# Four edits to a graph-network kernel on one core: bias copies, bf16 adjacency rows, casts on GpSimd, a merged first loop

## The chip, the core and the metric

One core of a Trainium2 chip runs the whole program. The metric is the device time in microseconds (us), lower is better. The core has a matrix engine (TensorE, PE in the rows), its weight loads (PEld), VectorE (DVE), ScalarE (ACT), GpSimd (POOL) and a queue engine (SyncE, SP) that here issues nearly all DMAs. The engines meet only at semaphores.

## The reference, cut to what matters

2708 nodes with 256 features are padded to 22 blocks of 128 (NT = 22). Four graph layers follow one another, each behind a layer norm and a ReLU with a residual sum; the fourth is run only if a test on the adjacency values asks for it, and here it does not.

```
# layer 0: attention of 4 heads of 64 columns over all neighbours
ht = (h @ Wm).reshape(n, 4, 64); el, er = ht . al, ht . ar
attn = softmax(where(adj == 0, -inf, leaky_relu(el[:, None] + er[None, :])))
out = attn @ ht
# layer 1: two GRU cells around an attention of 3 heads
node_support = (adj without diagonal) @ h
edge_output = gru(node_support, h, edge_Wih, edge_Whh, edge_bih, edge_bhh)
edge_support = mean over 3 heads of softmax(where(adj > 0, e_plus[None, :], NEG)) * adj @ (h @ W_head)
node_output = gru(edge_support, h, node_Wih, node_Whh, node_bih, node_bhh)
out = de * edge_output + dn * node_output
# gru(x, h): r, z = sigmoid(x @ Wih.T + bih + h @ Whh.T + bhh); n = tanh(xn + bin + r * (hn + bhn)); (1-z) n + z h
# layer 2: out = concat(h, adj @ h / (deg + 1)) @ W.T
```

## The kernel before, in words

The order of work on every engine is written out by hand: each engine has one stream of instructions with waits on named semaphores, and a wait holds everything behind it on that engine. The adjacency is held in AT as fp8, one block row per source block j.

**Layer 0.** First the features are normed and multiplied (L1628, L1641), and GpSimd casts the first 6 of the 22 column blocks of each adjacency row from f32 in STG to fp8 in AT (L693). Then comes a loop over the 22 source blocks that makes MOV, the operand of the attention products as two f16 halves: VectorE multiplies (L1145, `t_b`), GpSimd multiplies (L707, `t_d`), ScalarE rounds to the high half (L851), VectorE subtracts to the low half (L1139, `mov`). Only when all 22 are made do the attention units start. There are 12 units, 3 column groups of 6, 8 and 8 blocks times 4 heads, each with 22 steps j; unit n and step j make m = 22 n + j. One step: a threshold tile (fp8) of the scores, on ScalarE (L869) or VectorE (L1161) as `threshold_on_act` says, then two masks on VectorE (L1193 and, by xor, L1199), then four matmuls of 65 columns for each block (L1674). Of the thresholds, ScalarE makes all of unit 0, 13 of 22 in units 1 to 7 and 18 in units 8 to 11. At j = 8 ScalarE evicts the unit before (L881) and VectorE normalizes it (L1208 to L1214, `head_out`). ScalarE also casts the 44 adjacency tiles of the second and third column group (L859), spread over units 0 to 7 by `casts_at`. In units 8 to 11 VectorE widens the adjacency (L1220) and GpSimd clears its diagonal blocks (L715). The scores of a unit are loaded by SP (`load_el`) two units ahead.

**Layer 1, edge loop.** 22 blocks t. Per block PE does half of a support product (L1720, 44 matmuls of 256 columns), the head products (L1732, L1734), and the gates of the GRU (`gru_mm`): 12 matmuls of 512 columns (L1759), one of 3 rows that adds the bias (L1761), then twice 6 of 256 columns (L1766), each with a bias matmul (L1767). ScalarE takes tanh of the gates (L940), VectorE combines (L1388, L1390), ScalarE takes tanh (L942), GpSimd subtracts (L728, `delta`), VectorE blends (L1397, L1398), GpSimd adds to X (L733, L734, `apply`). VectorE also splits support and products into halves (L1342, L1348, L1351). Between these VectorE takes row maxima (L1366): each of the 3 heads needs, for 22 rows in two halves, the maximum of the adjacency half row (f32, 704 KB, loaded from the input for every head anew, three buffers AROW) times the scores of the head (EB). Of the 132 maxima 44 are done by block 13 (`ROWS_SPLIT`), 73 by the end of the loop (`ROWS_EDGE`), the rest at every second step of the attention. GpSimd clears the diagonal block of one half of each row first (L743). In block 20 the maxima of head 0 are turned on PE (L1778), copied (L1379), saved and reloaded broadcast (`save_maxima`, `load_maxima`); the first attention unit needs them.

**Layer 1, attention.** 9 units of 22 steps. Per step: exponents (L952 on ScalarE or L1409 on VectorE), a mask (L1419), powers (L961), and 2 matmuls of 257 columns for each block (L1812, L1813). Six pieces of the next weights are split on GpSimd (L675 to L677). The node bias is summed and split in three bf16 parts on VectorE at m = 118 to 120 (L1271 to L1282). VectorE counts sensitive entries (L1471) from m = 122.

**Node GRU and layer 2.** 22 blocks of `gru_mm` again, with ScalarE's `node_high` (L993), VectorE's `support_half` (L1526), norm statistics (L1062) and, from block 10, the linear product of layer 2 (L1853) in between. Then the neighbour sums (L1866).

## Time and profile before

| what | us |
|---|---|
| median of the runs (3) | 1363.55 |
| lowest, highest | 1361.31, 1370.84 |
| the profiled execution's own time | 1376.85 |
| its span (first to last instruction) | 1375.0 |
| granted TensorE clock, mean over the span | 0.935 of full |
| busy in the span: PE, VectorE, ScalarE, GpSimd | 1187.0, 1000.2, 759.6, 267.6 |

The rows further down come from that one execution; times in them are us from the start of its span. In a timeline row the first number is the start, the second the duration, and a bracket at the end tells how long the engine was idle before and what released it. VectorE's instructions overlap a little at their ends, so the distance between two starts is what one costs.

### The profile page before, as it was taken

To read this page: it belongs to the slowest core of one execution; us is meant where nothing else is said; L and a number is where in the kernel's file an instruction comes from. 1 tells how busy PE (TensorE), PEld (TensorE's weight loads), DVE (VectorE), ACT (ScalarE), POOL (GpSimd) and SP (SyncE) were. 2 spreads that over 40 slices of the span, in tenths; PEclk is the share of its full clock that TensorE was granted. 3 is DMA by queue.
4 is the path that set the end of the run, shared out by engine and by line. 5 is a ranking of instruction groups with operands and counts; after the bars stand their busy time and mean duration, and the time that the engine had idled before them with its cause. 6 is when DMAs were issued, how large, how long until landed. Compare 5 with 4: busy or idle time off the path is not lost.

```text
span 1375.0 us, 36177 instructions
## 1 busy us (share of the span) xinstructions
PE 1187.0 (86%) x15179; PEld 944.5 (69%) x15179; DVE 1000.2 (73%) x2281; ACT 759.6 (55%) x1142; POOL 267.6 (19%) x340
## 2 busy tenths in 40 slices
PE   4518897999868999999966999997899998988996
PEld 3418897999757766566635888886788654446885
DVE  6587997999985676676776999898995365553641
ACT  3469987998752122222116999896989225553000
POOL 4730000032041022332231110111210042220000
PEclk9759999999975999999977999999999999999998
DMA  9715553211015667768679778676762000020532
GB/s 319 240 70 170 180 148 119 81 34 65 3 49 210 211 205 252 245 215 285 223 251 344 228 247 329 208 248 210 257 223 101 1 28 20 16 92 1 190 107 84
DMA packets 88623, 223.59 MB, mean 163 GB/s; under 512 B 7427, under 2 KB 52345, under 8 KB 88197
## 3 DMA queue, kind: packets, MB, share of 16 engines
q1 hardware_dynamic: 87269, 220.68, 48.5%
q8 instruction: 121, 1.98, 0.6%
q10 hardware_dynamic: 1184, 0.53, 0.1%
q14 instruction: 49, 0.40, 0.1%
HBM read 201.45 MB, written 19.73 MB: 161 GB/s over the span
## 4 chain that ended last, share of the span: by engine, by line
PE 52%; DMA 15%; DVE 14%; ACT 8%; POOL 5%; issue 4%; SPq 1%; DVEq 0%; ACTq 0%; POOLq 0%
PE PS L1674 12%; DMA arena<-in_adj 12%; PE PS L1812 10%; PE PS L1813 10%; PE PS L1866 8%; ACT arena L869 3%; PE PS L1759 3%; DVE scratch L1366 3%; PE PS L1853 2%; PE PS L1766 2%; DVE arena L1139 1%; ACT AT L859 1%; POOL X L734 1%; PE PS L1709 1%; DVE arena L1199 1%
## 5 line engine op out<-in xcount | busy, mean ns | idle before, releaser
L1812 PE MATMUL PS<-arena 128*128 128x257 f16 x1452 | 331.5, 276 | 27.3 <-ACT arena L961 21.6
L1813 PE MATMUL PS<-arena 128*128 128x257 f16 x1452 | 331.3, 278 | 0.0
L1674 PE MATMUL PS<-arena 128*128 128x65 f16 x7744 | 261.8, 196 | 76.1 <-DVE arena L1199 61.4
L1674 PEld LDWEIGHTS PS<-arena 128*128 128x128 fp8e4 x7744 | 258.1, 99 | 79.7 <-issue 59.0
L1366 DVE CUSTOM_DVE_ANT_0 scratch<-arena 128x1408 bf16<-128x1408 f32 x132 | 216.9, 1643 | 84.1 <-DMA arena<-in_adj 48.5
L961 ACT ACTIVATE arena<-arena 128x896 int16<-128x896 uint8 (+1 forms) x198 | 187.4, 972 | 36.3 <-DVE arena L1419 27.5
L869 ACT ACTIVATE arena<-arena 128x1024 fp8e4<-128x1024 f32 (+1 forms) x185 | 189.9, 1089 | 17.7 <-DVE arena L1193 16.9
L1812 PEld LDWEIGHTS PS<-arena 128*128 128x128 bf16 x1452 | 144.2, 99 | 52.8 <-ACT arena L961 18.1
L1813 PEld LDWEIGHTS PS<-arena 128*128 128x128 bf16 x1452 | 141.6, 97 | 23.1
L952 ACT ACTIVATE arena<-arena,E1B 128x896 uint8<-128x896 f32 (+1 forms) x131 | 139.2, 1063 | 13.6 <-DMA arena<-m_rows 13.6
L942 ACT ACTIVATE arena<-arena 128x256 f32<-128x256 f32 x44 | 18.3, 416 | 205.0 <-DVE arena L1390 205.0
L1193 DVE TENSOR_TENSOR arena<-arena,AT 128x256 int32<-128x256 int32 (+1 forms) x264 | 104.8, 397 | 25.3 <-ACT arena L869 18.2
L1759 PE MATMUL PS<-arena 128*128 128x512 f16 x528 | 123.0, 383 | 0.0
L1720 PE MATMUL PS<-AT,arena 128*128 128x256 fp8e4 x968 | 112.1, 276 | 0.0
L1866 PE MATMUL PS<-arena,AT 128*128 128x256 f16 x968 | 106.2, 273 | 0.8 <-DVE X L1520 0.8
L1199 DVE TENSOR_TENSOR arena<-arena,AT 128x256 int32<-128x256 int32 (+1 forms) x264 | 104.1, 395 | 0.0
L1720 PEld LDWEIGHTS PS<-AT,arena 128*128 128x128 f16 x968 | 94.2, 99 | 14.0
L1866 PEld LDWEIGHTS PS<-arena,AT 128*128 128x128 fp8e4 x968 | 94.6, 98 | 12.5 <-DVE X L1520 1.1
L743 POOL TENSOR_TENSOR arena<-arena,NOTI 128x128 f32<-128x128 f32 x66 | 46.0, 697 | 286.2 <-DMA arena<-in_adj 286.1
L1759 PEld LDWEIGHTS PS<-arena 128*128 128x128 f16 x528 | 52.3, 99 | 56.5 <-issue 2.5
L1419 DVE TENSOR_TENSOR arena<-arena,AT 128x224 int32<-128x224 int32 (+1 forms) x198 | 79.8, 428 | 10.8 <-ACT arena L952 10.6
L728 POOL TENSOR_TENSOR arena<-arena 128x256 f32<-128x256 f32 x44 | 32.8, 745 | 256.1 <-ACT arena L942 256.1
(192 smaller groups left out, 1570.7 us busy)
## 6 DMA issues: line engine op xcount, KB each, us to landing
arena<-in_adj SPq DMA_DIRECT2D x176, 704.0 KB, 5.3
arena<-in_adjT SPq DMA_DIRECT2D x44, 512.0 KB, 4.2
hw_saved<-arena SPq DMA_DIRECT2D x22, 387.0 KB, 7.5
arena<-in_adjT SPq DMA_DIRECT2D x22, 384.0 KB, 4.9
arena<-hw_saved SPq DMA_DIRECT2D x9, 774.0 KB, 7.7
arena<-h_saved SPq DMA_DIRECT2D x44, 128.0 KB, 2.1
arena<-e_rows SPq DMA_DIRECT2D x3, 1408.0 KB, 7.1
arena<-el_rows SPq DMA_DIRECT2D x8, 512.0 KB, 5.5
```

What stands on the lines that cost most here:

```text
L869: act.activation(THR[:, m % NTHR, 0:nb * P], ELB[:, n % 2, 0:nb * P], ACT.Sigmoid, bias=ERB[:, j, h:h + 1], scale=SHARP, saturate=False).t ...
L952: act.activation(Y[:, m % NRING, 0:nb * P], MB[n % 2][:, 0:nb * P], ACT.Relu, bias=E1B[:, j * H1 + h:j * H1 + h + 1], saturate=False).then ...
L961: act.activation(PWb[:, m % NRING, 0:nb * P], Y[:, m % NRING, 0:nb * P], ACT.Copy, scale=256.0).then_inc(sem("p_ready"), 1)
L1193: dve.tensor_tensor(mask_words(m, 0), THRi[:, m % NTHR, 0:GA[g][1] * P // 4], adj_words(m), ALU.bitwise_and).then_inc(sem("m_plus"), 1)
L1199: dve.tensor_tensor(mask_words(m, 1), mask_words(m, 0), adj_words(m), ALU.bitwise_xor).then_inc(sem("masks_built"), 1)
L1366: dve.tensor_tensor_reduce(junk, AROW[:, L % 3, :], eb[:, c * QUARTER:(c + 1) * QUARTER], 1.0, 0.0, ALU.mult, ALU.max, M2[:, t, c, h:h + 1 ...
L1674: ins = pe.matmul(PS[:, k, q * C0:(q + 1) * C0], MASK[:, (m + j) % NMASK, q, k * P:(k + 1) * P], MOV[:, j, 2 * h + q, a, :], start=(j == 0 ...
L1720: ins = pe.matmul(PS[:, c, 0:D], HHL[:, j, a, c * P:(c + 1) * P], AT[:, j, i0 * P:i1 * P], start=(j == 0 and a == 0), stop=(j == NT - 1 an ...
L1759: pe.matmul(PS[:, bank, :], half(c, a), w[:, c, b, 0:2 * D], start=(first and c == 0 and a + b == 0), stop=False)
L1812: pe.matmul(PS[:, k, 0:D + 1], weights, w[:, 0:D + 1], start=(j == 0), stop=False)
L1813: ins = pe.matmul(PS[:, k, 0:D + 1], weights, w[:, D + 2:2 * D + 3], start=False, stop=(j == NT - 1))
L1866: ins = pe.matmul(o, AT[:, j, t * P:(t + 1) * P], YHL[:, j, a, :], start=(j == 0 and a == 0), stop=(j == NT - 1 and a == 1))
```

## The change

1. **First loop merged.** The loop that makes MOV is no longer ahead of the units: VectorE does `weighted(m+2)` and `low_part(m)` ahead of the mask of step m of unit 0, ScalarE does `weighted_high(j+2)` ahead of the threshold of step j.
2. **Casts on GpSimd.** The 44 casts of adjacency tiles go from ScalarE to GpSimd, in order, after its MOV work; SP loads 11 tiles a unit in units 0 to 3. The thresholds of units 1 to 11 are made by ScalarE except where j % 7 = 3 (3 of 22).
3. **bf16 rows.** In units 4 to 10 the adjacency rows are staged (66 pieces of 8, 7 and 7 blocks, two f32 buffers RST), cast to bf16 on GpSimd with the diagonal cleared (two buffers RSH), and saved to a DRAM tensor. The row maxima then load bf16 half rows (352 KB, two buffers) without GpSimd's part. One load serves heads 0 and 1 in the edge loop, which now takes 88 maxima in blocks 0 to 19; the 44 of head 2 follow in the attention, one at every 2.5 steps from m = 0. Heads 0 and 1 are turned and saved together.
4. **Bias copies.** The bias matmuls go. The summed bias is broadcast to 128 partitions, ScalarE copies it into the PSUM banks two blocks ahead (512 columns for r and z, 512 for n), and all gate matmuls accumulate on it. Seven matmuls of 512 columns (`open_bank`) open the banks once. The three-part split of the bias on VectorE goes.

```diff
-            return j % 5 not in (1, 3) if n < 2 * H0 else j % 5 != 3
+            return j % 7 != 3
...
+            def save_row(i):
+                t, g = row_pieces[i]
+                b0, nb = G0[g]
+                sp.wait_ge(sem("row_cast"), i + 1)
+                sp.dma_start(AH_D[t, :, b0 * P:(b0 + nb) * P], RSH[:, i % 2, 0:nb * P]
+                             ).then_inc(sem(f"ws_out{2 + i % 2}"), 16)
+            def stage_row(i):
...
+                if i == 0:
+                    sp.wait_ge(sem("stg_used"), len(chunk0) - NT)
+                if i >= 2:
+                    sp.wait_ge(sem("row_cast"), i - 1)
+                sp.dma_start(RST[:, i % 2, 0:nb * P], t_in["adj"][t * P:(t + 1) * P, b0 * P:(b0 + nb) * P]
+                             ).then_inc(sem(f"raw{2 + i % 2}"), 16)
+                if i >= 1:
+                    save_row(i - 1)
             for u in range(len(units0)):
                 for j in range(NT):
-                    if (u, j) in casts_at and casts_at[(u, j)] + 4 < len(chunk0):
-                        load_chunk(casts_at[(u, j)] + 4)
+                    n = NT + 11 * u + j // 2 + 4
+                    if u < 4 and j % 2 == 0 and n < len(chunk0):
+                        load_chunk(n)
+                    i = 10 * (u - 4) + j // 2
+                    if u >= 4 and j % 2 == 0 and j < 20 and i < len(row_pieces):
+                        stage_row(i)
                     if j == 20 and u + 2 < len(units0):
                         load_el(u + 2)
...
             def load_row(L):
-                h, t, c = row_of(L)
-                if L >= 3:
-                    sp.wait_ge(sem("rmax"), L - 2)
-                sp.dma_start(AROW[:, L % 3, :], t_in["adj"][t * P:(t + 1) * P, c * QUARTER:(c + 1) * QUARTER]
-                             ).then_inc(sem(f"arow{L % 3}"), 16)
+                t, c = half_of(L)
+                if L >= 2:
+                    sp.wait_ge(sem("rmax"), maxima_after(L - 2))
+                sp.dma_start(AROW[:, L % 2, :], AH_D[t, :, c * QUARTER:(c + 1) * QUARTER]
+                             ).then_inc(sem(f"arow{L % 2}"), 16)
...
@@ gpsimd
+            pool.wait_ge(sem("mov"), NT)
+            for n in range(NT, len(chunk0)):
+                g, j = chunk0[n]
+                b0, nb = GA[g]
+                pool.wait_ge(sem(f"stg{n % 4}"), 16 * (n // 4 + 1))
+                pool.tensor_copy(AT[:, j, b0 * P:(b0 + nb) * P], STG[:, n % 4, 0:nb * P], saturate=False
+                                 ).then_inc(sem("stg_used"), 1)
+            for i, (t, g) in enumerate(row_pieces):
+                b0, nb = G0[g]
+                pool.wait_ge(sem(f"raw{2 + i % 2}"), 16 * (i // 2 + 2))
+                if i >= 2:
+                    pool.wait_ge(sem(f"ws_out{2 + i % 2}"), 16 * (i // 2 + 1))
+                if b0 <= t < b0 + nb:
+                    blk = RST[:, i % 2, (t - b0) * P:(t - b0 + 1) * P]
+                    link(pool.tensor_tensor(blk, blk, NOTI[:], ALU.mult))
+                pool.tensor_copy(RSH[:, i % 2, 0:nb * P], RST[:, i % 2, 0:nb * P]).then_inc(sem("row_cast"), 1)
...
@@ scalar
+            def gate_bias_rz(t, base, bias):
+                act.activation(PS[:, gates_bank(t, base), :], bias[:, 0:2 * D], ACT.Copy).then_inc(sem("bias_rz"), 1)
+            def gate_bias_n(t, base, bias):
+                act.activation(PS[:, gates_bank(t, base) + 2, :], bias[:, 2 * D:4 * D], ACT.Copy).then_inc(sem("bias_nb"), 1)
...
                 act.activation(trz[:, t % 2, :], PS[:, gates_bank(t, base), :], ACT.Tanh, scale=0.5 / WSCALE).then_inc(sem("trz"), 1)
+                if t + 2 < NT:
+                    act.wait_ge(sem("trz"), base + t + 1)
+                    gate_bias_rz(t + 2, base, bias)
                 act.wait_ge(sem("u"), base + t + 1)
                 act.activation(gt[:, t % 2, :], gt[:, t % 2, :], ACT.Tanh, scale=1.0 / WSCALE).then_inc(sem("n"), 1)
+                if t + 2 < NT:
+                    gate_bias_n(t + 2, base, bias)
...
@@ vector
+            weighted(0)
+            weighted(1)
             for m in range(last + 1):
                 n, j = divmod(m, NT)
+                if m + 2 < NT:
+                    weighted(m + 2)
+                if m < NT:
+                    low_part(m)
                 positive_mask(m)
...
@@ tensor
+            def open_bank(bank, data):
+                pe.matmul(PS[:, bank, :], identh[:], data, start=True, stop=True).then_inc(sem("opened"), 1)
...
-                pe.matmul(PS[:, bank, :], ones3[0:3, :], bias[0:3, 0:2 * D], start=False, stop=True).then_inc(sem("rz_mm"), 1)
...
-                    ins = pe.matmul(o, ones3[0:3, :], bias[0:3, (2 + q) * D:(3 + q) * D], start=False, stop=True)
```

## Rows read from the trace of the kernel before

**Rows 1.** Windows: length; busy us of PE, PEld, DVE, ACT, POOL; clock; DMA share.
```profile
92.30:116.40 24.10, 16.45 (x432) 16.35 (x432) 13.96 (x45) 24.10 (x29) 0.00 (x0) 0.77 0.45 134
116.40:175.80 59.40, 52.70 (x1550) 51.50 (x1551) 56.15 (x175) 58.28 (x95) 0.00 (x0) 0.97 0.56 169
201.50:224.70 23.20, 20.00 (x615) 19.62 (x612) 23.06 (x59) 22.89 (x36) 0.00 (x0) 1.00 0.56 162
279.00:303.80 24.80, 23.48 (x734) 23.23 (x730) 24.66 (x61) 22.79 (x36) 8.52 (x7) 1.00 0.14 41
...
459.70:700.60 240.90, 228.91 (x1607) 151.60 (x1606) 170.49 (x309) 48.00 (x118) 66.63 (x86) 0.99 0.72 238
...
928.00:970.00 42.00, 31.40 (x261) 25.76 (x259) 36.17 (x56) 29.36 (x33) 7.17 (x6) 0.92 0.64 224
```
**Rows 2.** Timeline of unit 5: thresholds on ScalarE, masks and a threshold on VectorE.
```profile
217.65 3.22 ACT L869 ACTIVATE arena<-arena 128x1024 fp8e4<-128x1024 f32 x3
...
218.71 0.42 DVE L1193 TENSOR_TENSOR arena<-arena,AT 128x256 int32<-128x256 int32 x1
219.04 0.74 DVE L1161 TENSOR_SCALAR arena<-arena 128x1024 fp8e4<-128x1024 f32 x1
219.71 0.42 DVE L1199 TENSOR_TENSOR arena<-arena,AT 128x256 int32<-128x256 int32 x1
```
**Rows 3.** Timeline of the loop that makes MOV: one of its 22 turns.
```profile
83.40 0.41 DVE L1145 TENSOR_TENSOR arena<-AT,arena 128x260 f32<-128x260 f32 x1
...
83.74 1.11 DVE L1139 TENSOR_TENSOR arena<-arena 128x520 f16<-128x520 f32 x1
...
84.77 0.42 DVE L1145 TENSOR_TENSOR arena<-AT,arena 128x260 f32<-128x260 f32 x1
```
**Rows 4.** VectorE beside casts of GpSimd, in the timeline and by line (ns min/median/max).
```profile
L1145 DVE TENSOR_TENSOR arena<-AT,arena x22: 414/416/1049, 54.8 to 88.9; 128x260 f32<-128x260 f32 x22
L693 POOL CAST AT<-arena x22: 824/829/1073, 17.6 to 59.7; 128x768 fp8e4<-128x768 f32 x22
...
1000.62 1.09 POOL L676 CAST arena<-arena 128x768 f16<-128x768 f32 x1
1000.96 1.00 DVE L1419 TENSOR_TENSOR arena<-arena,AT 128x224 int32<-128x224 int32 x1
```
**Rows 5.** DMA issues: KB each, median us from issue to landing.
```profile
arena<-in_adjT SPq DMA_DIRECT2D x44, 512.0 KB, 4.2
...
arena<-e_rows SPq DMA_DIRECT2D x3, 1408.0 KB, 7.1
```
**Rows 6.** Timeline of one gate product in the edge loop, weight loads on PE.
```profile
529.19 2.37 PEld L1759 LDWEIGHTS PS<-arena 128*128 128x128 f16 x12
532.29 0.55 PEld L1766 LDWEIGHTS PS<-arena 128*128 128x128 f16 x6 [0.23 <-issue]
...
534.24 4.70 PEld L1720 LDWEIGHTS PS<-AT,arena 128*128 128x128 f16 x44
```
**Rows 7.** Row maxima as a group of lines, and a blend that waited for GpSimd.
```profile
L1366 DVE CUSTOM_DVE_ANT_0 scratch<-arena 128x1408 bf16<-128x1408 f32 x132 | 216.9, 1643 | 84.1 <-DMA arena<-in_adj 48.5 <-POOL arena L743 26.2 <-DMA arena<-e_rows 6.4
716.73 0.66 DVE L1397 SCALAR_TENSOR_TENSOR arena<-arena 128x256 f32<-128x256 f32 x1 [0.61 <-POOL arena L728]
```
**Rows 8.** Timeline from block 19 of the edge loop to the attention.
```profile
700.63 0.41 DVE L1388 SCALAR_TENSOR_TENSOR arena<-arena,PS 128x256 f32<-128x256 f32 x1
...
713.52 0.28 DVE L1379 COPY ET<-PS 22x128 f32<-22x128 f32 x1
...
728.36 0.37 PE L1812 MATMUL PS<-arena 128*128 128x257 f16 x1 [9.02 <-ACT arena L961]
```
**Rows 9.** Timeline: head 2's scores issued, and the first row maximum of the attention.
```profile
734.13 0.42 SPq L512 DMA_DIRECT2D arena<-e_rows  x1
...
735.34 1.62 DVE L1366 CUSTOM_DVE_ANT_0 scratch<-arena 128x1408 bf16<-128x1408 f32 x1 [3.37 <-POOL arena L743]
```
**Rows 10.** Timeline of one node block: VectorE's idle time before the next combine.
```profile
1111.10 0.42 DVE L1388 SCALAR_TENSOR_TENSOR arena<-arena,PS 128x256 f32<-128x256 f32 x1 [1.15 <-PE PS L1767]
```

More of the change, by code:

```diff
@@ L163, in gnn_stack_kernel @@
         HTF = AT[:, :, htf_at:htf_at + 4 * H0 * C0].bitcast(F32)
+        ar = Arena()
+        ar.at = stg_at
+        RST = ar.take(2, 1024)
+        RSH = ar.take(2, 1024, dt=BF16, size=2)
+        assert ar.at <= stg_end
         THRi = THR.bitcast(mybir.dt.int32)
@@ L220, in gnn_stack_kernel @@
         WHH2S = a2.take(DC, 2, 3 * D, dt=F16, size=2)
-        BIAS2 = a2.take(4 * D, dt=BF16, size=2)
+        BIAS2 = a2.take(4 * D)
         W2S = a2.take(DC, 2, 2 * D, dt=F16, size=2)
@@ L225, in gnn_stack_kernel @@
         tmp.at = rows_at
-        BR2 = tmp.take(4 * D)
         BRB2 = tmp.take(2 * D)
@@ L519, in _ @@
                     load_halves(GWS, 0, "we")
-            for L in range(3):
+            for L in range(2):
                 load_row(L)
@@ L579, in _ @@
                         load_products(0, c)
-            for L in range(ROWS_EDGE, ROWS_EDGE + 3):
+            for L in range(2 * NT, 2 * NT + 2):
                 load_row(L)
@@ L749, in _ @@
                     delta(t, 0, HR, GT)
-                    for L in range(rows_before(t + 1), rows_before(t + 2)):
-                        clear_diagonal(L)
                 if t >= 1:
@@ L847, in _, with weighted_high @@
             act.wait_ge(sem("coef"), 1)
-            for t in range(NT):
+            def weighted_high(t):
                 act.wait_ge(sem("t_b"), t + 1)
@@ L1009, in _ @@
             node_high(0)
+            act.wait_ge(sem("bias_n"), 1)
+            act.wait_ge(sem("opened"), 8)
+            for t in range(2):
+                gate_bias_rz(t, NT, BIAS2)
+                gate_bias_n(t, NT, BIAS2)
             for t in range(STEPS):
@@ L1140, in low_part, with weighted @@
                                   MOV[:, t, :, 0, :], ALU.subtract).then_inc(sem("mov"), 1)
-            for t in range(NT):
+            def weighted(t):
                 if t >= 3:
@@ L1876, in _ @@
             pe.wait_ge(sem("ht_back"), 16)
+            for bank in range(1, 5):
+                open_bank(bank, HTN[:, 0, :])
             early = NORM2[-1][0]
```

297 lines of the change are left out of this document (129 added, 168 removed).

## The prediction

> **What bounds the kernel now.** I read the page's busy shares first, then the windows by stage, then in each stage the timeline, to see which engine has no gaps. The windows [rows 1] are to be read as length against the busy time of each engine. In layer 0 it is VectorE: unit 5 (window 201.5 to 224.7) has 23.06 us of VectorE in 23.2 and only 20.00 of PE; unit 8 (279.0 to 303.8) has 24.66 in 24.8. In the edge loop of layer 1 (459.7 to 700.6) it is PE, 228.9 of 240.9, with VectorE at 170.5 and the DMA engines at 0.72. The attention is PE's except at its start and from 928 to 970, where PE is idle for 10.6 of 42 us. In the node loop PE is full too, but VectorE has little spare time in its chain [rows 10].
>
> Layer 0 can be counted. One mask costs the distance of two starts, 0.33 us, and a threshold of 1024 elements on VectorE 0.67 [rows 2]. Unit 5 has 44 masks (14.7), 9 thresholds (6.0) and the normalization of one unit (2.5, estimated from its five instructions of up to 0.7 us): 23.2, which is its length [rows 1]. Unit 8 has 4 thresholds (2.7), 7 widenings (3.8), so 23.7; what is left to 24.8 is what the seven small GpSimd instructions there take from VectorE. So VectorE's own work plus what GpSimd takes from it gives the length.
>
> What GpSimd takes is in [rows 3, 4]. A multiply of 0.42 us on VectorE took 1.049 when a cast of 768 elements ran on GpSimd beside it: 0.63 lost to an instruction of 0.83. A mask of the attention of 896 columns took 1.00 beside another cast of 768 (larger masks take 0.42). A cast of 1024 thus takes about 0.85 us of VectorE, one of 896 0.75.
>
> **Part 1, the merged first loop.** A turn of the old loop costs 1.37 us [rows 3]; 22 make 30.1, and unit 0 takes 24.1 [rows 1]: 54.2 us. Merged, VectorE does in a turn the same 1.37 (GpSimd's share is already in it) and two masks of 768 columns, 0.27 each (0.33 scaled to 192 words plus the fixed part), so 1.91; 22 turns are 42. ScalarE's 1.5 us a turn stay beside it. The saving of 12 is cut by about 5, because the first threshold needs scores whose load SP issues behind the front's (4.2 us for such a size, [rows 5]) and whose wait was hidden by the old loop. **-7** (bounds -12 and 0).
>
> **Part 2, casts and thresholds.** Units 1 to 3 took 59.4 us [rows 1]. VectorE's own work becomes 44 x 0.27 + 3 x 0.53 + 2.1 = 15.5 each, 46.5. GpSimd's casts in them are 15, 11 and 11, since SP loads four ahead and eleven a unit: 37 x 0.85 = 31.5. Sum 78: **+19**. ScalarE, rid of casts but with 19 thresholds of 1.04 (three in 3.22 us with the last lasting 1.14, [rows 2]), would need 18 to 19 here and 23.4 in later units, so it is no bound. GpSimd may lag, but not for long: SP's queue is in order, and the scores of unit 4 stand behind the load that needs 33 casts, so a starved GpSimd stops the thresholds, and VectorE then waits. Bounds: from -5 (casts fit in gaps, ScalarE's 18 a unit) to +22.
>
> **Part 3a, making the bf16 rows.** In units 4 to 10 VectorE's own work falls to 44 x 0.33 + 3 x 0.67 + 2.5 = 19.2, with widenings and statistics 153 for the seven; before they took 184. GpSimd adds 7 last casts (6), 58 row pieces of mean 0.78 (45) and 19 diagonal blocks of 0.21 (4), less some 13 that fit beside normalizations and statistics: 195, +11. But there is a second limit, the round trip of the pieces. Two f32 buffers: a piece is loaded only when the one two before is cast, behind the store in between on SP. That is 0.8 to issue both, 4.2 to land [rows 5], 1.04 to cast and some 0.5 of waiting for the port, 6.6 for two pieces, 3.3 each. The scores of unit u+2 stand in SP behind the pieces of unit u, so unit 11 can't start before 59 pieces are through: about 187 (first piece staged) + 5 + 59 x 3.3 + 5 = 392, where the port sum gives 383 and the old trace has 360. I take 388, that is **+16** beyond parts 1 and 2. Unit 11 then holds 7 pieces more and all 22 diagonal blocks in place of 8: **+8**. The later loads of layer 1 stand behind the pieces on SP too. Bounds for both: 0 (the round trip alone with landings of 3.5 us) and +40.
>
> **Part 4, bias copies in the edge loop.** From the first 512-column load to the first 256-column load are 3.10 us for 12 matmuls, and 1.95 for the rest up to the next support product [rows 6]. Without the three bias matmuls 24 matmuls at their usual pace need 2.60 and 1.30, so 1.15 us a block go from PE, and 11.7 becomes 10.56. What is late next is VectorE. Its rows: 4.4 maxima a block of 1.6 [rows 7] are 7.1 (44 in 13 blocks, 3.4 a block, before); bf16 rows need no fewer elements and the scores stay f32, so I give them no speed. With splits, combine and blend (3.5) that is 10.65. When VectorE never waits, GpSimd's subtraction stands behind the first maximum and the blend waits 0.6 to 0.7 for it [rows 7]; the update of X takes 0.2 more. 11.55 a block, 231 in blocks 0 to 19, plus 4.5 at the start, since the second maximum now needs the scores of head 1 whose load comes behind those of head 0 (7.1 us each alone, [rows 5]), plus 2 for loads with two buffers, ends at 236.6 where 240.9 were: **-4**. Waits for row loads (48.5 us) and diagonals (26.2) of VectorE go [rows 7], but they lay mostly beside PE. Bounds: -25 (PE alone) and +5.
>
> From the combine of block 19 to the attention's first matmul are 27.7 us; 12.9 of them to the copy of the maxima, in which VectorE and PE wait for rows, and 14.9 from there [rows 8], which stay. With no maxima after block 19 the copy comes about 4.8 after the combine: **-8**.
>
> **Attention.** At m = 0 the first maximum is now head 2's. The scores of head 2 are issued at 734.1 and land in 7.1 [rows 5, 9], at 741.2; the maximum before ran at 735.3. VectorE stands there and the masks behind it, so PE, which used up its two ready tiles, waits **+6** more. Against it the three-part bias split on VectorE before 940 becomes two instructions, and the stop of 10.6 us in 928 to 970 [rows 1] with the late maxima of head 2 should nearly go: **-12** with a few smaller stops. Sum -6, bounds -13 and +6. PE sets the rest, so 15 fewer maxima are worth nothing there.
>
> **Node loop.** PE saves 1.15 a block again. But VectorE is idle only 1.15 us before its combine [rows 10], and ScalarE's new copy of 512 columns (about 0.55, half of a 1024-column threshold of [rows 2]) stands between the tanh and the high half that VectorE waits for, so 0.6 is left: 11 plain blocks, -6.6. In the other 11, which wait on norms, ScalarE has more work and I take nothing. Seven opening matmuls and four first copies cost 2: **-4**, bounds -17 and +4. The same copies and openings ahead of the edge loop: **+2**.
>
> **Sum.** -7 + 19 + 16 + 8 - 4 - 8 - 6 - 4 + 2 = +16 on 1376.85, the profiled execution's own time, gives 1393. That execution lies 1% above the median of the runs, 1363.55; in the same proportion, 1379 (+1.2%).
>
> A rule of the Trainium skill bears on the largest term. What the trace shows is a loss of 0.63 us beside a cast of 0.83 [rows 4]. SBUF — State Buffer, section SBUF: two separate sides, says that the port pair which VectorE and GpSimd share is an exclusive lock held for the whole instruction, and that the loser fully blocks. By that each of the 110 casts would take its whole 1.04 and not 0.85, 21 us more, and the sum would be 1400.
>
> **Rivals.** (A) GpSimd's casts cost VectorE little. For it: in dense stretches GpSimd waits, not VectorE, if VectorE wins the port. Against it: [rows 4], and SP's queue, which ties the scores to the casts. Then units run at ScalarE's and PE's pace, layer 0 is limited by the round trip of the pieces alone and ends where it did (-2), the edge loop is nearly PE's (-20), and with -8, -6, -4, +2 the sum is -38: 1339, or 1326 as a median. It decides if layer 0 ends before about 400. (B) Half of it: the port costs what I say, but pieces land faster than 4.2 us in a quiet stretch of DMA, and layer 0 loses 18 in place of 36: -2, or 1362. (C) The cast blocks VectorE for its whole duration, as [rows 4] would allow if the 1.00 us of the attention's mask is the rule and the 0.63 of the multiply luck: 102 casts at 0.19 more, +19, 1398 as a median; it decides if masks beside casts of 1024 take over 1.4 us. (D) The change does not do what it says: the bias copy comes late and PE waits for it in each block. ScalarE has 48 us in 240.9 [rows 1], so I give it next to nothing.
>
> **Chances.** Forecast 0.50, A 0.25, B 0.17, C 0.08. A measurement of this kernel can tell about 1% from no change. The forecast is slower by over 1% in three of four of its cases, C always; A is faster; B is the same in most cases. So faster 0.28, same 0.24, slower 0.48. The range holds most of A and C: 1325 to 1410; the forecast's own is 1362 to 1398.
>
> **What would show it.** Right: the matmul L1674 still runs after 410 us; masks of 0.42 us that take about 1.2 beside casts of 1024 in units 1 to 10; units 5 to 7 of 27 us or more, units with SP's pieces 3.3 us apart; edge blocks of 11.4 to 11.8 with VectorE full; PE's stop at the attention's start of 12 us; no stop at 940. Wrong: layer 0 ending before 395, or edge blocks of 10.6; then A holds.

## The result: slower by 5.4%, and the profile after

The kernel before took 1366.41 us in the median of four runs beside it (1361.31 to 1370.84), the changed kernel 1440.86 (1435.06 to 1446.7). The ratio is 1.0539 with a 95% interval of 1.0495 to 1.0583. The profiled execution has a span of 1443.5 us where [rows 1] came from one of 1375.0. The stretches of the two traces differ by:

| stretch | before, us | after, us | difference | predicted |
|---|---|---|---|---|
| span's start to the end of unit 0 | 116.4 | 118.9 | +2.5 | -7 |
| units 1 to 3 | 59.4 | 76.6 | +17.2 | +19 |
| units 4 to 10 | 184.4 | 248.3 | +63.9 | +16 |
| unit 11 | 27.2 | 32.6 | +5.4 | +8 |
| last mask to the first gate tanh of layer 1 | 74.7 | 75.0 | +0.3 | +2 |
| tanh of edge blocks 0 to 19 | 228.6 | 223.7 | -4.9 | -4 |
| from there to the attention | 37.6 | 23.4 | -14.2 | -8 |
| attention | 351.9 | 353.8 | +1.8 | -6 |
| node loop and the last sums | 294.7 | 291.2 | -3.6 | -4 |

One row carries most of the miss: units 4 to 10, with 48 of 52 us. Each trace is one execution, and code that two kernels share differs between their traces too: with the bias copies alone, layer 0 is that of the kernel before, and its units 4 to 11 took 205 us where [rows 1]'s trace has 211.6. A few us in one row are no finding. The windows of the kernel after are read against those of [rows 1]: unit 0, units 1 to 3, unit 5, unit 8, the edge loop, and the attention's start.

```profile
core 0: us, PE busy (x) PEld busy (x) DVE busy (x) ACT busy (x) POOL busy (x), PEclk, DMA share, GB/s
68.90:118.90 50.00, 23.34 (x432) 21.37 (x432) 32.49 (x83) 30.65 (x43) 11.54 (x19) 0.57 0.06 22
118.90:195.50 76.60, 58.93 (x1554) 57.38 (x1555) 76.19 (x157) 56.94 (x95) 53.24 (x38) 0.88 0.80 271
221.70:254.50 32.80, 25.87 (x798) 25.46 (x794) 23.49 (x53) 21.54 (x35) 15.24 (x11) 0.98 0.61 186
330.70:365.00 34.30, 24.86 (x704) 23.99 (x704) 31.31 (x60) 23.50 (x37) 13.93 (x14) 0.93 0.76 231
548.90:775.10 226.20, 210.23 (x1534) 149.45 (x1533) 204.12 (x340) 67.94 (x156) 54.77 (x54) 0.98 0.42 118
798.50:818.00 19.50, 5.71 (x34) 4.17 (x35) 5.88 (x11) 3.33 (x5) 3.40 (x5) 0.62 0.75 236
```

Units 1 to 3 are VectorE's (76.19 of 76.60), as predicted. Unit 0 is not: VectorE works 32.49 of 50. Nor is unit 5, where VectorE is busy 23.49 of 32.80 and no engine is full. What is waited for there stands in the groups of units 4 to 10 (GpSimd's with unit 11), ScalarE's threshold L879, GpSimd's cast of a row piece L751 and VectorE's first mask L1229:

```profile
L879 ACT ACTIVATE arena<-arena 128x1024 fp8e4<-128x1024 f32 x136 | 145.2, 1170 | 83.5 <-DMA arena<-el_rows 61.9 <-DVE arena L1229 21.1
...
L751 POOL CAST arena<-arena 128x896 bf16<-128x896 f32 (+1 forms) x66 | 96.1, 1458 | 103.9 <-DMA arena<-in_adj 102.3
...
L1229 DVE TENSOR_TENSOR arena<-arena,AT 128x256 int32<-128x256 int32 x154 | 82.9, 538 | 51.6 <-ACT arena L879 51.6
```

The thresholds wait 61.9 us for the scores (el_rows), and the masks 51.6 for the thresholds. SP's own line shows why the scores are late. L443 is the load of a unit's scores, L499 a row piece's load, L489 its store:

```profile
281.81 0.32 SPq L489 DMA_DIRECT2D adj_rows_half<-arena  x1
282.17 0.43 SPq L499 DMA_DIRECT2D arena<-in_adj  x1
283.33 0.32 SPq L489 DMA_DIRECT2D adj_rows_half<-arena  x1
283.75 0.38 SPq L443 DMA_DIRECT2D arena<-el_rows  x1
284.17 0.87 SPq L499 DMA_DIRECT2D arena<-in_adj  x1
```

The scores of unit 7 are issued at 283.75, right behind the tenth piece of the group before them, and unit 7 starts at 293.1. It is so for each: loads at 246.9, 283.8, 322.0, 355.8, 396.5 and 430.4, unit starts at 254.5, 293.1, 330.7, 365.0, 405.0 and 443.8. A unit lasts about as long as ten pieces.

The turn of the merged loop in unit 0, one timeline for each engine:

```profile
89.19 0.42 DVE L1184 TENSOR_TENSOR arena<-AT,arena 128x260 f32<-128x260 f32 x1
89.52 0.69 DVE L1177 TENSOR_TENSOR arena<-arena 128x520 f16<-128x520 f32 x1
91.13 0.36 DVE L1229 TENSOR_TENSOR arena<-arena,AT 128x192 int32<-128x192 int32 x1 [0.92 <-ACT arena L879]
91.41 0.35 DVE L1235 TENSOR_TENSOR arena<-arena,AT 128x192 int32<-128x192 int32 x1
91.68 0.42 DVE L1184 TENSOR_TENSOR arena<-AT,arena 128x260 f32<-128x260 f32 x1
...
89.64 0.65 ACT L869 ACTIVATE arena<-arena 128x520 f16<-128x520 f32 x1 [1.03 <-DVE arena L1184]
90.19 0.91 ACT L879 ACTIVATE arena<-arena 128x768 fp8e4<-128x768 f32 x1
```

From one weighted (L1184) to the next are 2.49 us. ScalarE waits for it, makes the high half (L869), then the threshold (L879); the mask (L1229) waits 0.92 us for that, and the next weighted stands behind the masks on VectorE. It is a ring through two engines, and neither is full.

### The profile page after: what moved, and what is told of

It is laid out like the page before. It is cut to its first block, busy times and chain, and to the rows that moved or that the text cites. A ratio compares the mean times of both kernels' runs of the same rounds, so it can differ in the third digit from the quotient of the medians.

```text
span 1443.5 us, 36050 instructions
## 1 busy us (share of the span) xinstructions
PE 1174.8 (81%) x15054; PEld 965.1 (67%) x15054; DVE 1025.2 (71%) x2216; ACT 808.6 (56%) x1232; POOL 380.1 (26%) x405
## 4 chain that ended last, share of the span: by engine, by line
PE 38%; DVE 21%; DMA 18%; POOL 9%; ACT 7%; issue 6%; SPq 1%; DVEq 0%; ACTq 0%; POOLq 0%
PE PS L1841 10%; PE PS L1842 10%; DMA arena<-in_adj 8%; DVE scratch L1396 8%; PE PS L1895 7%; DMA arena<-in_adjT 4%; PE PS L1791 3%; POOL AT L740 2%; POOL arena L751 2%; POOL arena L769 2%; PE PS L1882 2%; DVE arena L1378 2%; DMA arena<-e_rows 2%; DVE arena L1235 2%; ACT arena L879 1%
## 5 line engine op out<-in xcount | busy, mean ns | idle before, releaser
L1700 PE MATMUL PS<-arena 128*128 128x65 f16 x7744 | 286.9, 202 | 138.2 <-DVE arena L1235 131.8
L1700 PEld LDWEIGHTS PS<-arena 128*128 128x128 fp8e4 x7744 | 278.4, 103 | 146.7 <-DVE arena L1235 114.6
L879 ACT ACTIVATE arena<-arena 128x1024 fp8e4<-128x1024 f32 (+1 forms) x231 | 231.4, 1085 | 109.5 <-DMA arena<-el_rows 61.9
L1396 DVE CUSTOM_DVE_ANT_0 scratch<-arena 128x1408 bf16<-128x1408 bf16 x132 | 223.1, 1690 | 30.1 <-DMA arena<-e_rows 22.5
L1229 DVE TENSOR_TENSOR arena<-arena,AT 128x256 int32<-128x256 int32 (+1 forms) x264 | 134.0, 507 | 75.0 <-ACT arena L879 75.0
L769 POOL TENSOR_TENSOR arena<-arena 128x256 f32<-128x256 f32 x44 | 47.2, 1072 | 378.4 <-ACT arena L964 378.4
L1235 DVE TENSOR_TENSOR arena<-arena,AT 128x256 int32<-128x256 int32 (+1 forms) x264 | 130.7, 496 | 0.0
L751 POOL CAST arena<-arena 128x896 bf16<-128x896 f32 (+1 forms) x66 | 96.1, 1458 | 103.9 <-DMA arena<-in_adj 102.3
```

The lines of the kernel that those rows point to most:

```text
L879: act.activation(THR[:, m % NTHR, 0:nb * P], ELB[:, n % 2, 0:nb * P], ACT.Sigmoid, bias=ERB[:, j, h:h + 1], scale=SHARP, saturate=False).t ...
L1229: dve.tensor_tensor(mask_words(m, 0), THRi[:, m % NTHR, 0:GA[g][1] * P // 4], adj_words(m), ALU.bitwise_and).then_inc(sem("m_plus"), 1)
L1235: dve.tensor_tensor(mask_words(m, 1), mask_words(m, 0), adj_words(m), ALU.bitwise_xor).then_inc(sem("masks_built"), 1)
L1396: dve.tensor_tensor_reduce(junk, AROW[:, L % 2, :], eb[:, c * QUARTER:(c + 1) * QUARTER], 1.0, 0.0, ALU.mult, ALU.max, M2[:, c, h * NT + t ...
L1700: ins = pe.matmul(PS[:, k, q * C0:(q + 1) * C0], MASK[:, (m + j) % NMASK, q, k * P:(k + 1) * P], MOV[:, j, 2 * h + q, a, :], start=(j == 0 ...
```

## The experiments

Two theories on the main loss: SP's in-order queue ties the scores to the pieces, or the port that GpSimd's casts share with VectorE slows the masks. Two on unit 0: the ring, or VectorE's own work. Beside them stands the question what each part is worth alone. Ratios are to the kernel before.

### The bias copies alone

Onto the kernel before: the wide BIAS rows, `bias_sum`, `gate_bias_rz`, `gate_bias_n`, `open_bank` and the new `gru_mm` of the change, and nothing else of it.

```
+                pe.wait_ge(sem("bias_rz"), base + t + 1)
...
-                pe.matmul(PS[:, bank, :], ones3[0:3, :], bias[0:3, 0:2 * D], start=False, stop=True).then_inc(sem("rz_mm"), 1)
```

> The kernel before with the bias copies alone (three-instruction sums, full-width bias rows, ScalarE's copies into PSUM, no bias matmuls); f32 rows, casts and first loop as before. Theory 1: in the old edge loop PE is the bound and VectorE has room (170 us in 241), so the 1.15 us a block go from the end: edge loop 20 to 24 us shorter, node loop 4 shorter as in the changed kernel, 1340 to 1345 us, about 0.983 of the kernel before. Theory 2: the f32 rows of 704 KB (DMA engines at 0.72 busy there) or ScalarE's two copies take over as soon as PE gives way: edge loop shorter by 8 at most, 1355 to 1360. Theory 3: what the changed kernel gained in the edge loop and behind it (19 us) came from its paired maxima and not from the biases: no more than 4 us here.

Measured: 1353.96 us, ratio 0.9888 (0.9826 to 0.9951). From the tanh of block 0 to the attention's first matmul 253.8 us in place of 266.2, the attention 5.5 shorter, the node loop and what follows 6.4. The plain edge blocks are 10.65 us apart, near the 10.56 counted from [rows 6], but over blocks 0 to 19 only 9.2 us are saved of the 20 that this makes, and the distances of many later blocks are 11.5 to 13.2. There VectorE waits 28.9 us for f32 rows and 22.5 for their diagonals. So theory 2 has the edge loop nearly right. The total lies between the two: theory 1 forecast a ratio of 0.983, theory 2 1355 to 1360 us where 1364 were (0.994 to 0.997), and the measured ratio is 0.9888. Theory 3 (no more than 4 us) is out, and with it the prediction's rival D, in which PE waits for the copies.

### Without the row pieces

The three other parts of the change on the kernel before: casts by GpSimd, threshold shares of the change, merged loop, bias copies; f32 rows by one head.

> The changed kernel without its bf16 rows (f32 rows, one head a load, as before); bias copies, casts on GpSimd and the merged first loop stay. Theory 1 (the pieces' queue): the row pieces cost layer 0 nearly all that units 4 to 11 lost, so these fall back to the old 211.6 us or a few below (one threshold a unit less on VectorE), unit 0 stays at 50 and units 1 to 3 at 77; last mask at 395 to 403, hence 1345 to 1362 with the edge loop of the run with bias copies alone. Theory 2 (port and ScalarE): the cast and threshold split are what slows units 4 to 11, and they stay above 240 us, 1390 or more.

Measured: 1367.22 us, ratio 0.9989 (0.9957 to 1.0022). Units 4 to 11, and then the masks of units 1 to 3 with casts beside them:

```profile
201.00:399.50 198.50, 183.87 (x5604) 181.76 (x5600) 181.25 (x489) 183.79 (x276) 28.36 (x15) 0.98 0.09 28
```

```profile
L1215 DVE TENSOR_TENSOR arena<-arena,AT 128x192 int32<-128x192 int32 x67 | 40.0, 596 | 0.0
L1209 DVE TENSOR_TENSOR arena<-arena,AT 128x192 int32<-128x192 int32 (+1 forms) x67 | 34.9, 521 | 0.0
```

Units 4 to 11 take 198.5 us, 13 less than before and 82 less than in the changed kernel. Units 1 to 3 take 23 more (82.3 where 59.4 were), and layer 0 ends at 399.5 where it ended at 387.4; what the bias copies save behind it makes the whole level. The difference of 5% to the changed kernel is thus the third part, the row pieces with the paired maxima: 82 us lost in units 4 to 11, some 14 of them given back between the edge loop's start and the attention. The bound of 1362 was passed by 5 us.

### Scores' loads issued by ScalarE

```
-                    if j == 20 and u + 2 < len(units0):
-                        load_el(u + 2)
...
+                if n + 2 < len(units0):
...
+                    act.wait_ge(sem("t_act"), act_thr[(n + 1) * NT])
...
+                    act.dma_start(ELB[:, n % 2, 0:nc0 * P].rearrange("p (k q) -> p k q", q=P),
+                                  EL_D[c0:c0 + nc0, h2, :].partition_broadcast(P)).then_inc(sem(f"elb{n % 2}"), 16)
```

> The changed kernel with one edit: the loads of the next scores (el_rows, units 2 to 11) are issued by ScalarE behind its last threshold of a unit, and no longer by SP behind ten row pieces. Theory 1 (SP's queue): units 5 to 10 take 26 to 28.5 us each in place of 33 to 40 (the sum of VectorE's own work and the port), waits of the threshold for el_rows go, last mask near 430 in place of 476. But the pieces still come 3.8 us apart and end near 457, and GpSimd's diagonal blocks and the first casts of layer 1 stand behind them, so the whole gains 5 to 20 us only: 1420 to 1435. Theory 2 (the port): the casts hold VectorE, and the units stay above 33 with masks late after thresholds that are ready; 1435 to 1445.

Measured: 1407.1 us, ratio 1.027 (1.0209 to 1.0332), 34 us below the changed kernel; more than expected. Units 4 to 10 take 202.7 us in place of 248.3: units 5 to 9 24.6 to 31.3 each, but unit 10 37.6, where 26 to 28.5 were expected of all. What holds unit 10 was not followed. The last mask ends at 436.8, the last piece is cast at 446.9, and the first cast of layer 1 is at 456.4, 20 us behind the mask. The queue is shown: this edit changes only who issues the scores' loads, and it takes 46 of the 64 us back. The forecast's sum of VectorE's work and the port, 195, is near what was left.

### The threshold first

```
+                    if threshold_on_act(n, j):
+                        threshold(n, j)
                     if n == 0 and j + 2 < NT:
                         weighted_high(j + 2)
-                    if threshold_on_act(n, j):
-                        threshold(n, j)
```

> The changed kernel with one edit: in unit 0 ScalarE makes a block's threshold first and the weighted high half of two blocks on behind it. Theory 1 (a chain through three engines): a turn of 2.50 us is weighted, high half, threshold and mask one after another; with the threshold first the chain spans two turns, and a turn costs 1.9 to 2.1: unit 0 takes 41 to 45 us in place of 50. The whole gains 5 to 9 us, for the casts and pieces behind it start that much earlier. Theory 2 (VectorE's own work with the port in it sets the turn): unit 0 stays at 49 to 51 and the time at that of the changed kernel.

Measured: 1422.77 us, ratio 1.039 (1.0325 to 1.0455), 18 us below the changed kernel. Unit 0 takes 38.6 us, and a turn on VectorE's timeline has no gap:

```profile
87.41 0.42 DVE L1184 TENSOR_TENSOR arena<-AT,arena 128x260 f32<-128x260 f32 x1
87.75 0.69 DVE L1177 TENSOR_TENSOR arena<-arena 128x520 f16<-128x520 f32 x1
88.36 0.34 DVE L1229 TENSOR_TENSOR arena<-arena,AT 128x192 int32<-128x192 int32 x1
88.63 0.77 DVE L1235 TENSOR_TENSOR arena<-arena,AT 128x192 int32<-128x192 int32 x1
89.32 0.42 DVE L1184 TENSOR_TENSOR arena<-AT,arena 128x260 f32<-128x260 f32 x1
```

1.91 us, the number that the prediction had worked out for VectorE. In unit 0 the ring was the whole difference, 11.4 us. The whole gained more than the 5 to 9 expected, because units 4 to 10 took 239.7 us in place of 248.3; why they did was not followed.

### Bias copies and the reordered merged loop on the kernel before

Casts stay with ScalarE, but none in unit 0, whose columns the operand's source still covers.

```
-        for u, count in enumerate((6, 6, 5, 5, 6, 6, 5, 5)):
+        for u, count in enumerate((0, 8, 7, 7, 6, 6, 5, 5)):
...
-                casts_at[(u, 1 + 4 * i if i < 2 else 10 + 3 * (i - 2))] = n
+                casts_at[(u, 1 + 4 * i if i < 2 else 9 + 2 * (i - 2))] = n
```

> The kernel before with the bias copies and the merged first loop, its threshold ahead of the high half as in the run before; rows in f32, casts on ScalarE, none of them in unit 0 now but 8, 7 and 7 in units 1 to 3 (then 6, 6, 5, 5 as before). Theory 1 (the chain is cut and ScalarE bears the casts): first loop and unit 0 together 38 to 41 us in place of 54.2; units 1 to 3 are ScalarE's (39 thresholds of 0.93, 22 casts of about 0.95, 36 evictions of 0.33: 69 us) and take 67 to 71 in place of 59.4; the rest as with the bias copies alone; 1340 to 1350 where that run had 1354. Theory 2: the casts moved together into units 1 to 3 delay masks by more than the merge gains, or unit 4 waits for its casts: 1354 or more.

Measured: 1345.56 us, ratio 0.9827 (0.9763 to 0.9891). That interval overlaps the one of the bias copies alone, so what the merge adds is read from the trace: unit 0 ends at 107.0 in place of 116.4. Units 1 to 3 take 61.6 us, and ScalarE is full in them as expected, though I had counted 67 to 71:

```profile
107.00:168.60 61.60, 55.66 (x1584) 54.34 (x1584) 56.22 (x175) 61.60 (x100) 0.00 (x0) 0.93 0.69 213
...
L866 ACT ACTIVATE arena<-arena 128x768 fp8e4<-128x768 f32 (+1 forms) x41 | 38.5, 1012 | 0.0
L856 ACT ACTIVATE AT<-arena 128x1024 fp8e4<-128x1024 f32 x23 | 25.8, 1122 | 0.0
L878 ACT ACTIVATE arena<-PS,arena 128x65 f32<-128x65 f32 x36 | 7.7, 363 | 0.0
```

By count times mean duration these make 80 us in 61.6, so ScalarE's instructions overlap at their ends: an eviction of 0.36 us starts 0.20 before the next in the median, a threshold of 0.99 us 0.83, a cast of 1.11 us 0.95. The distance of two starts, not the duration, is what a full engine is to be counted by.

### Both edits and a third buffer in the changed kernel

```
-        RST = ar.take(2, 1024)
+        RST = ar.take(3, 1024)
...
-                if i >= 1:
-                    save_row(i - 1)
+                if i >= 2:
+                    save_row(i - 2)
```

> The changed kernel with both edits of the runs before (scores' loads issued by ScalarE, threshold first) and a third: three f32 buffers for the row pieces in place of two, each store one piece later on SP. Theory 1 (round trip and queue were the loss of units 4 to 11, the port the rest): pieces 2.2 to 2.7 us apart where GpSimd gets the port, all through near 360 to 385; unit 0 of 39 us, units 1 to 3 of 77 to 83, units 4 to 11 of 225 to 240; last mask 415 to 425, first cast of layer 1 within 10 us behind it (it was 20 in the run with scores by ScalarE); 1378 to 1390. Theory 2: loads of the pieces and the scores then share the DMA engines and land late, or the denser casts hold VectorE longer: 1395 or more, about what the two edits give alone.

Measured: 1394.08 us, ratio 1.0183 (1.0128 to 1.0238), just above the range given. The pieces come 2.63 us apart in the median (3.33 in the changed kernel) and the last is cast at 393. But units 4 to 10 take 213.8 us, with masks of 0.53 us beside denser casts.

### Casts of adj_T by GpSimd alone, and the same with fills

The first is the kernel before with the casts and threshold shares of the change alone. The second replaces each of these casts; the adjacency of its later groups is all ones then.

```
-                pool.tensor_copy(AT[:, j, b0 * P:(b0 + nb) * P], STG[:, n % 4, 0:nb * P], saturate=False)
+                pool.memset(AT[:, j, b0 * P:(b0 + nb) * P].bitcast(mybir.dt.int32), 0x38383838)
```

> The kernel before with the casts of adj_T on GpSimd and the new share of thresholds alone; old first loop, f32 rows, bias matmuls. Theory 1 (the port): VectorE full in units 1 to 3 with masks of 0.5 to 0.6 us in place of 0.33, units 1 to 3 of 78 to 84 us (59.4 before), units 4 to 11 of 196 to 202 (211.6 before), so +9 to +12 in all, 1372 to 1390 by the chip's clock. Theory 2: the casts fit beside VectorE and the 82 us of the run without row pieces came from the merge that ran ahead of the loads: units 1 to 3 under 70.

> The run with the casts on GpSimd alone, and each cast replaced by a fill of the same 1024 bytes with ones as 256 words: it reads nothing and converts nothing, so the adjacency of the later groups is left out and is all ones; waits, loads and order are the same. Theory 1 (the port, by the duration of GpSimd's instruction): fills last 0.2 to 0.4 us, masks go back towards 0.33, units 1 to 3 take 58 to 63 us. Theory 2 (loads of 512 KB gate STG, SP's queue and with them scores and masks; DMA share 0.81 there): they stay above 72 us.

Measured, one execution each: 1370.77 and 1358.56 us. With casts units 1 to 3 take 71.7 us, less than expected, because with the old loop 15 of the 44 casts are done when unit 1 starts; units 4 to 11 take 199.7 (196 to 202 expected). So +12 and -12: GpSimd's casts of adj_T move time between units and cost layer 0 nothing in all, as far as two single traces can tell (against the 205 us above, units 4 to 11 gain only 5). With fills the masks are back at 0.36 us, but units 1 to 3 take 66.9, between the theories:

```profile
L710 POOL MEMSET AT<- 128x256 int32 x29 | 9.3, 319 | 51.6 <-DMA arena<-in_adjT 51.6
```

```profile
L1183 DVE TENSOR_TENSOR arena<-arena,AT 128x192 int32<-128x192 int32 x56 | 19.9, 356 | 19.2 <-ACT arena L861 13.1 <-PE PS L1664 6.0
```

GpSimd waits 51.6 us for chunks of 512 KB, so once the port is free, the supply of chunks and the scores behind them in SP's queue are the likely bound of these units; no run takes them away. The port costs the masks their time, but only 5 of the 12 us of these units go with it; the other 7.5 stay when the casts are fills.

### The two edits without the third buffer, and with late maxima

The second moves the 44 maxima of head 2 by six tiles.

```
-        row_at = {5 * i // 2: 2 * NT + i for i in range(2 * NT)}
+        row_at = {6 + 5 * i // 2: 2 * NT + i for i in range(2 * NT)}
```

> The changed kernel with the scores' loads issued by ScalarE and the threshold first, without the third buffer of the mended run. Theory 1 (the third buffer gave nothing, since by then VectorE and the port set the units and not the round trip): the time of the mended run within 0.5%, 1388 to 1398, units 4 to 10 together 200 to 216 us as with three buffers (213.8), though the last piece is cast 20 us or more later than there (393). Theory 2 (the round trip still counts): 1403 or more, the last mask later than 436.

> The run with the two edits, and the 44 row maxima of head 2 six tiles later in the attention, so that VectorE's first masks don't stand behind one that waits for the scores of head 2. Theory 1: PE's stop of 14.1 us at the attention's start falls to 5 to 7 (5.9 in the kernel before), the attention is 7 to 9 us shorter (344 to 346 us from first to last matmul), and the time 7 to 9 below the run with the two edits. Theory 2: PE then waits for its first tiles in another way (masks behind the checks, maxima of head 0), or the stop moves to tile 6: less than 3 us.

Measured: 1398.83 us, ratio 1.0226 (1.0168 to 1.0285), and 1386.78 us, ratio 1.0132 (1.0087 to 1.0176). With two buffers the last piece is cast at 438, 45 us later than with three, and units 4 to 10 take 195.4: the third buffer is worth nothing that can be told. What it saves in pieces, the masks pay. Nor do the two edits' gains add: 34 and 18 us each alone, 42 together. With late maxima the stop of 13.9 us at the attention's start becomes two, 1.4 and 3.2, and first to last matmul is 340.9 us in place of 352.2, more than expected. What that stop was stands in VectorE's group of the changed kernel from 798 to 820:

```profile
L1396 DVE CUSTOM_DVE_ANT_0 scratch<-arena 128x1408 bf16<-128x1408 bf16 x3 | 4.9, 1619 | 11.7 <-DMA arena<-e_rows 11.7
```

### Row pieces as fills

The run with the two edits, its casts of pieces replaced; the rows that the maxima read are left out and are all ones.

```
-                pool.tensor_copy(RSH[:, i % 2, 0:nb * P], RST[:, i % 2, 0:nb * P]).then_inc(sem("row_cast"), 1)
+                pool.memset(RSH[:, i % 2, 0:nb * P].bitcast(mybir.dt.int32), 0x3F803F80).then_inc(sem("row_cast"), 1)
```

> The run with the two edits, and GpSimd's cast of each row piece replaced by a fill of the same bf16 piece with ones, so that the rows of the maxima are left out and are all ones; loads, stores, waits and diagonal multiplies stay. Theory 1 (the port, priced by the duration of GpSimd's instruction): fills of 0.25 to 0.4 us in place of casts of 1.04; masks go from 0.53 back towards 0.40, and units 4 to 10 take 168 to 182 us in place of 203 to 214. Theory 2 (what slows VectorE there is the transfers' writes to its memory, or the diagonals): masks stay near 0.5 and the units near 200.

Measured, one execution: 1378.24 us, 20.6 below the run with the casts. The groups from 188 us to the end of unit 10, first with casts, then with fills:

```profile
L1235 DVE TENSOR_TENSOR arena<-arena,AT 128x256 int32<-128x256 int32 (+1 forms) x176 | 89.7, 510 | 5.5 <-ACT arena L877 5.5
L1241 DVE TENSOR_TENSOR arena<-arena,AT 128x256 int32<-128x256 int32 (+1 forms) x175 | 80.8, 462 | 0.0
```

```profile
L1235 DVE TENSOR_TENSOR arena<-arena,AT 128x256 int32<-128x256 int32 (+1 forms) x163 | 68.8, 422 | 37.1 <-ACT arena L877 27.2 <-PE PS L1706 9.8
L1241 DVE TENSOR_TENSOR arena<-arena,AT 128x256 int32<-128x256 int32 (+1 forms) x163 | 68.1, 418 | 0.0
L1106 DVE BATCH_NORM_STATS2 scratch<-X 128x6 f32<-128x256 f32 x14 | 5.9, 420 | 0.0
...
L748 POOL TENSOR_TENSOR arena<-arena,NOTI 128x128 f32<-128x128 f32 x20 | 38.1, 1906 | 47.5 <-DMA arena<-in_adj 47.5
L749 POOL MEMSET arena<- 128x448 int32 (+1 forms) x59 | 32.4, 553 | 91.4 <-DMA arena<-in_adj 90.2
```

The masks go from 0.51 and 0.46 to 0.42, as theory 1 said, and yet units 4 to 10 take 194.9 us, as long as the 195.4 with casts: expected were 168 to 182. VectorE now waits 37 us for ScalarE and PE. The port is what VectorE's masks lose their time to, but another bound stands right under it, by these rows ScalarE's 24 us a unit and PE's pauses. GpSimd isn't free of VectorE either: its diagonal multiplies take 1.9 us in the mean. What the whole gained came behind these units: unit 11 takes 6 us less, and the first cast of layer 1 is at 424.4 in place of 447.4, as GpSimd is done with its pieces sooner.

### Checks six tiles later

Onto the fastest kernel so far, that with the bias copies and the reordered loop.

```
-    CHECK_FIRST = 122
+    CHECK_FIRST = 128
```

> The fastest kernel so far (the kernel before with bias copies and the merged, reordered first loop), and the 26 loads and counts of adj rows in the attention begin six tiles later (at tile 128 in place of 122), so that they don't fill the DMA engines and SP's queue while the maxima of head 2 are stored and loaded. Theory 1: the load of m_rows lands earlier, PE's stops at the change to head 2 (1.7, 1.4 and 4.7 us) shrink to 1 to 4 in all, time 3 to 6 us less: 0.976 to 0.981 of the kernel before where it was 0.983. Theory 2: the store and load of the maxima take the same chain however quiet the DMA engines are: no change, 0.981 to 0.985.

Measured: 1337.71 us, ratio 0.9789 (0.9745 to 0.9833), which overlaps the interval without the edit (0.9763 to 0.9891); the trace tells more. The three stops at the change to head 2 (1.7, 1.4 and 4.6 us) are gone, not shrunk, and the attention takes 338.0 us from first to last matmul in place of 346.5. ScalarE's exponents there, in the kernel without the edit (925 to 945) and in this one (920 to 940):

```profile
L965 ACT ACTIVATE arena<-arena,E1B 128x1024 uint8<-128x1024 f32 x6 | 6.8, 1135 | 5.5 <-DMA arena<-m_rows 5.5
```

```profile
L965 ACT ACTIVATE arena<-arena,E1B 128x1024 uint8<-128x1024 f32 x8 | 9.1, 1132 | 0.0
```

This kernel beats both of the case, by 2.1% and 7%. It has two parts of the change, the first with its threshold moved ahead, and none of the other two; the later checks and the casts spread anew are its own.

## Why the prediction was wrong

The direction was right, and not by luck: units 1 to 3 lost what was forecast for them. The size was not: +16 us forecast, +68 on the trace, and 1440.86 lies above every rival and above the range's upper end, 1410. Rival A (casts cost little) is refuted by masks of 0.5 to 0.6 us in the mean; the pieces landed in 4.5 and 4.9 us, not faster than 4.2 as rival B wanted; C fails by its own sign, masks of over 1.4 us beside casts: the longest in the changed kernel's units took 1.26. Point by point:

- **The row pieces (+16 forecast, +63.9 measured): the step that failed.** It held two sums against each other for the start of unit 11, VectorE with the port (383) and the pieces' round trip (392), and set 388 between them. The first sum's number came out: once the scores leave SP's queue, and with two buffers, units 4 to 10 take 195.4 to 202.7 us where 195 was forecast. But the run with fills takes the same 194.9 without the casts' reads, so the agreement doesn't prove the port's share of it, and may be luck in part. The second sum is the one that governed, and its three terms were all low. The first piece was cast at 211.3, not 192: unit 4 started 8 us later than forecast, and the 44 chunk casts ended at 207. The pace was 3.33 us in the median, as forecast, but 3.78 in the mean, since some casts were held up for 3 to 5.4 us. The scores of unit 11 took 7.7 us to land behind the pieces, not 5. That makes 19 us for the start, 24 for the 59 pieces (218.7 us from the first cast to the issue of the scores, where 194.7 were forecast) and 3 for the landing. The last 6 of the 52 us between 392 and 443.8 were no term of the sum: the first threshold of unit 11 ran at 438.1, and its first mask 5.7 us later, behind the last masks of unit 10.
- What should have warned me stood in my own text: the scores of unit u+2 stand in SP behind the pieces of unit u. I used it for unit 11 only. It means that each unit lasts ten pieces, and a term that governs every unit has its mean to be priced, not its undisturbed case. The upper bound for this part and unit 11, +40, lay far below the 69.3 that the two rows measured.
- **The merged loop (-7, measured +2.5).** The sum of VectorE's work, 1.91 us, was exact. The step that failed was to let ScalarE's 1.5 us "stay beside it": I had added up each engine and not followed the order on ScalarE, where the high half of two blocks on stands ahead of the threshold that the mask waits for.
- **Units 1 to 3 (+19, measured +17.2)**: right, by VectorE's load and 0.85 us for a cast. The runs of the changed kernel and its edits hold 37 or 43 casts in these units and take 76.6 and 76.9 us, or 81.7 to 83.0; less the prediction's 46.5 for VectorE's own work, an estimate, that is 0.81 to 0.85 us a cast in each. The fills show that with the port free another bound would stand a few us lower.
- **Unit 11 (+8, measured +5.4)**: right.
- **Edge loop (-4, measured -4.9)**: right, with VectorE at 204 of 226 us in the window above. The start cost 6.3 (18.0 us for the first block, 11.7 before), 4.5 forecast; the blocks then come 10.65, later 10.9 and 12.7 apart, mean 11.4 with 11.55 forecast. The forecast's own terms (231, 4.5 and 2) add to 237.5 and not to the 236.6 that it gives, a slip of 0.9 us. bf16 rows made a maximum no faster:

```profile
L1396 DVE CUSTOM_DVE_ANT_0 scratch<-arena 128x1408 bf16<-128x1408 bf16 x78 | 135.2, 1734 | 4.3 <-DVE M L1396 4.3
```

- **Tail (-8, measured -14.2)**: the direction was right; undersized, since the last blocks, 16.1 and 21.4 us apart before, shrank to 13.3 and 9.95 as well.
- **Attention (-6, measured +1.8).** PE's stop at its start grew from 5.9 to 14.1 us, by 8.2 where 6 was forecast: from the issue of head 2's scores to the maximum that waits for them went 9.9 us. The -12 at the change to head 2 was mostly wrong: stops of 12.1 us there became 7.7. I had put them down to the bias split and late maxima, and that was one of four stops, the one of 3.9 us; it is gone in the run with bias copies alone too. The rest was the maxima's load behind the checks' loads of 704 KB, shown by moving the checks.
- **Node loop (-4, measured -3.6)**: right in sum. Its eight plain blocks (11 were counted) are 4.12 us apart in place of 5.22, 1.10 each with 0.6 forecast, so VectorE's chain wasn't next; some of the blocks with norms give part of it back (13.0 and 12.8 us where 10.2 and 11.9 were).
- **The Trainium skill's rule** of an exclusive lock held for the whole instruction (SBUF — State Buffer, section SBUF: two separate sides) had given 21 us more for the casts. By it, as an estimate, units 1 to 3 would take 46.5 + 37 x 1.04 = 85 us, and 91 with 43 casts; they took 76.6 and at most 83.0. The traces don't agree with the rule's size.

## What to carry to other kernels

When a change puts a paced stream of transfers into an in-order queue, every later load in that queue gets the stream's pace: price each stretch by the mean distance of the stream, disturbed casts included, or issue the urgent loads from another engine. When two loops are merged, follow the ring of waits through the engines in their issue order; the sum of work of the busiest engine is a lower bound only. A third buffer or a freed port was worth little here, because the next bound stood close below.

## What the runs showed of the hardware that I had not expected

The port between GpSimd and VectorE has two faces. Mostly each cast slows a mask beside it (from 0.41 to some 1.15 us). But in some stretches VectorE goes on at full speed and GpSimd stands. In the run with scores by ScalarE, GpSimd and then VectorE:

```profile
305.26 6.95 POOL L749 CAST arena<-arena 128x1024 bf16<-128x1024 f32 x1 [1.93 <-DMA arena<-in_adj]
```

```profile
305.20 0.74 DVE L1203 TENSOR_SCALAR arena<-arena 128x1024 fp8e4<-128x1024 f32 x1
305.87 0.41 DVE L1241 TENSOR_TENSOR arena<-arena,AT 128x256 int32<-128x256 int32 x1
...
310.90 0.41 DVE L1235 TENSOR_TENSOR arena<-arena,AT 128x256 int32<-128x256 int32 x1
311.23 1.52 DVE L1203 TENSOR_SCALAR arena<-arena 128x1024 fp8e4<-128x1024 f32 x1
```

A cast that takes 1.04 us lasted 6.95, while 16 masks ran at 0.33 us apart; it ended only in the next threshold, which took 1.52 us in place of 0.74. Ten such instructions of over 2.2 us, five casts and five diagonal multiplies, made 47 of GpSimd's 127 busy us up to the last piece. Why one stretch goes the one way and the next the other was not settled. It is where rival A's picture held. In the changed kernel eight casts of pieces of 2.4 to 5.4 us last 24 us longer than the usual 1.04, most of the 29 us by which the mean pace exceeds the median.

PE paid for its pauses again in its clock. In the kernel before, PE stood 3.9 us from 228.1, and two of the windows behind it show its granted clock:

```profile
235.00:240.00 5.00, 5.00 (x141) 5.00 (x140) 0.76 (x2) 4.15 (x16) 0.00 (x0) 0.85 0.02 3
240.00:245.00 5.00, 5.00 (x163) 5.00 (x160) 3.79 (x9) 5.00 (x6) 0.00 (x0) 1.00 0.35 108
```

141 matmuls in 5 us at a mean of 0.85 (part of the stretch at 1.2 GHz, part at 2.4), 163 at 1.00. In the changed kernel, where each unit begins with such a pause, the mean over units 4 to 11 is 0.88 where the kernel before has 0.97.
